# A four-layer mixer kernel: VectorE's y and z first in a step, ScalarE's high part of z before the exponential, chunk-end scaling one step sooner in the last steps

## The reference

```python
proj = hidden_states @ in_proj_w.T               # gate (8192), x|B|C (10240), dt (128)
hBC  = silu(conv1d(x|B|C, 4 taps, causal) + conv_b)
x, Bm, Cm = hBC as (H=128 heads, P=64), (G=8 groups, N=128), (G=8, N=128)
dt = softplus(dt + dt_bias);  A_dt = -exp(A_log) * dt;  x_dt = x * dt
Lmat   = exp(segment_sum(A_dt))                  # decay inside a chunk of 128 tokens
Y_diag = (Cm Bm^T * Lmat) x_dt                   # within the chunk
states = (Bm * exp(A_last - A_cumsum))^T x_dt    # state at the chunk's end
Y_off  = Cm states_of_previous_chunk * exp(A_cumsum)
y = Y_diag + Y_off + D * x
y = y * rsqrt(mean(y^2) + eps) * norm_w * silu(gate)
out = y @ out_proj_w.T
```

## Time and profile before

| what | value |
|---|---|
| median of 3 runs | 1646.56 us (1642.46 to 1646.75) |
| the profiled execution's own time | 1649.56 us |
| its span | 1647.8 us |
| TensorE matmul busy | 1592.1 us, 97% |
| VectorE busy | 1358.0 us, 82% |
| ScalarE busy | 1281.6 us, 78% |
| GpSimd busy | 801.7 us, 49% |
| one group, from one copy to `m_cb_across` to the next | 171.1 to 173.3 us |

### The profile page before, as it was taken

How to read it: one execution, slowest core, us unless ns; L and a number is a source line. 1 busy time by engine, 2 the same in 40 slices (tenths; PEclk the granted TensorE clock), 3 DMA queues, 4 the chain that set the end, 5 groups by cost and what they waited for, 6 DMA issues and landing times.

```text
span 1647.8 us, 27075 instructions
## 1 busy us (share of the span) xinstructions
PE 1592.1 (97%) x8984; PEld 1305.5 (79%) x8984; DVE 1358.0 (82%) x2199; ACT 1281.6 (78%) x2218; POOL 801.7 (49%) x806
## 2 busy tenths in 40 slices
PE   6999999999999999999999999999999999999988
PEld 5888777788888887888788788888788888888766
DVE  5887886888888888887888887898888888878766
ACT  4454459888989798979987898888888888798842
POOL 3565124554556455545554454544554555454460
PEclk9999999999999999999999999999999999999999
DMA  5320345455565446545555455545554645445321
GB/s 174 120 91 1 111 133 155 143 161 148 140 179 153 146 130 176 155 129 150 170 143 160 135 170 143 173 115 172 152 160 131 166 145 160 144 142 161 116 71 52
DMA packets 186074, 229.56 MB, mean 139 GB/s; under 512 B 22384, under 2 KB 122096, under 8 KB 184272
## 3 DMA queue, kind: packets, MB, share of 16 engines
q1 hardware_dynamic: 185936, 227.84, 46.6%
HBM read 190.02 MB, written 37.75 MB: 138 GB/s over the span
## 4 chain that ended last, share of the span: by engine, by line
PE 43%; DVE 20%; issue 9%; ACT 7%; DMA 7%; SPq 1%; POOL 1%; DVEq 0%; ACTq 0%; POOLq 0%
PE bank L160 8%; PE bank L162 7%; PE bank L161 7%; DVE m_xc L1955 7%; PE bank L2343 4%; PE bank L2347 4%; PE bank L2309 4%; PE bank L2344 4%; DMA m_x_rows<-x_turned_rows 4%; DMA x_turned_rows<-m_x_blocks 3%; DVE m_gate L1955 3%; ACT m_mt L1661 2%; DVE m_y L2047 2%; PE bank L2331 2%; DVE xdt L2000 1%
## 5 line engine op out<-in xcount | busy, mean ns | idle before, releaser
L160 PE MATMUL bank<-xh,w_h 128*128 128x512 f32 x1152 | 463.4, 402 | 6.9 <-DVE m_xc L1955 3.9
L162 PE MATMUL bank<-xh,w_l 128*128 128x512 f32 x1152 | 450.9, 391 | 0.0
L161 PE MATMUL bank<-xl,w_h 128*128 128x512 f32 x1152 | 450.5, 391 | 0.0
L1569 POOL TENSOR_TENSOR m_z_l<-m_zg,m_z_h 128x512 fp32r<-128x512 f32 x128 | 179.4, 1401 | 458.2 <-ACT m_z_h L1715 458.2
L1551 POOL TENSOR_TENSOR w_l<-w_raw,w_h 128x512 fp32r<-128x512 f32 x142 | 203.6, 1434 | 228.2 <-ACT w_h L1629 228.2
L1661 ACT ACTIVATE m_mt<-m_mt,m_unit 128x128 f32<-128x128 f32 x1024 | 312.3, 390 | 0.0
L160 PEld LDWEIGHTS bank<-xh,w_h 128*128 128x128 f32 x1152 | 217.1, 188 | 61.9 <-issue 18.9
L162 PEld LDWEIGHTS bank<-xh,w_l 128*128 128x128 f32 x1152 | 216.9, 188 | 46.1
L1955 DVE SCALAR_TENSOR_TENSOR m_xc<-bank,m_par_slots,m_xc 128x1020 f32<-128x1020 f32 (+2 forms) x192 | 243.9, 1270 | 9.9 <-ACT m_xc L1640 5.4
L161 PEld LDWEIGHTS bank<-xl,w_h 128*128 128x128 f32 x1152 | 217.4, 189 | 40.4
L2343 PE MATMUL bank<-m_wo_h,m_z_h 128*128 128x512 f32 x512 | 205.0, 400 | 9.2 <-ACT m_z_h L1715 8.6
(11 more groups left out here) (315 smaller groups left out, 2857.2 us busy)
## 6 DMA issues: line engine op xcount, KB each, us to landing
m_mt<-ncs_rows SPq DMA_DIRECT2D x128, 512.0 KB, 5.8
w_raw<-w_in SPq DMA_DIRECT2D x144, 256.0 KB, 4.2
x_turned_rows<-m_x_blocks SPq DMA_DIRECT2D x120, 256.0 KB, 3.9
m_x_rows<-x_turned_rows SPq DMA_DIRECT2D x480, 64.0 KB, 2.3
m_wo_raw<-w_out_in SPq DMA_DIRECT2D x64, 256.0 KB, 3.9
m_e<-ecs_rows SPq DMA_DIRECT2D x128, 128.0 KB, 3.7
a_wo_raw<-wo_in SPq DMA_DIRECT2D x8, 1024.0 KB, 5.0
x<-x_in SPq DMA_DIRECT2D x8, 256.0 KB, 4.3
```

What stands on the lines that cost most here:

```text
L160: nc.tensor.matmul(out, ah, bh, start=first, stop=False)
L161: nc.tensor.matmul(out, ah, bl, start=False, stop=False)
L162: return nc.tensor.matmul(out, al, bh, start=False, stop=last)
L1569: nc.gpsimd.tensor_tensor(z_l[:, s % 2, :, :], zg[:], f(z_h[:, s % 2, :, :]), ALU.subtract).then_inc(zl_ready, 1)
```

## The change

Three orders are changed; no instruction is added or taken away.

1. VectorE's step: the order was `times_dt`, first `turn_blocks`, `add_out`, then `make_y` and `make_z`. Now it is first `turn_blocks`, `make_y` and `make_z`, `add_out`, `times_dt`.
2. ScalarE's step: `decay` is split in `clamp` (the eight Relu) and `decay` (the exponential). In paired steps other than t = 1 the order is clamps, (in step 15 the copy to `m_cb_across`,) high part of z, square of y, exponential. Before it was clamps, exponential, (copy,) square, high part. In all steps the high part now comes before the square.
3. GpSimd's step: in the last eight steps of the last group `to_chunk_end` for an even step is called at the end of the odd step before it.

```diff
@@ gpsimd step
-                if s % 2 == 0 and own(kind):
+                if s % 2 == 0 and own(kind) and paired(kind, s):
                     to_chunk_end(g, s)
+                if s % 2 == 1 and turned_by_tensor(kind, s):
+                    to_chunk_end(g, s + 1)
@@ scalar
-            def decay(g, s):
+            def clamp(g, s):
                 g, s = g + s // STEPS, s % STEPS
                 half, t = divmod(s, NT)
                 act.wait_ge(rows_loaded[s % ROW_BUFS], (g * (STEPS // ROW_BUFS) + (s // ROW_BUFS + 1)) * 16)
...
                 last.then_inc(clamped, 1)
+
+            def decay(g, s):
+                g, s = g + s // STEPS, s % STEPS
                 act.wait_ge(clamped, at(g, s))
                 slot = mt[:, s % ROW_BUFS, :, :]
                 nc.scalar.activation(slot, slot, ACT.Exp, scale=-1.0).then_inc(decay_ready, 1)
@@
             def square_and_high(g, s):
+                act.wait_ge(z_ready, at(g, s))
+                act.wait_ge(out_done, at(g, s - 2))
+                nc.scalar.activation(z_h[:, s % 2, :, :], zg[:], ACT.Copy).then_inc(zh_ready, 1)
                 act.wait_ge(y_ready, at(g, s))
                 act.wait_ge(sq_summed, at(g, s - 1))
                 nc.scalar.activation(ysq[:], y[:], ACT.Square).then_inc(sq_ready, 1)
-                act.wait_ge(z_ready, at(g, s))
-                act.wait_ge(out_done, at(g, s - 2))
-                nc.scalar.activation(z_h[:, s % 2, :, :], zg[:], ACT.Copy).then_inc(zh_ready, 1)
@@ scalar step
-                if ahead(kind, s + 2) and not (kind == "lead" and s == STEPS - 1):
+                clamps = ahead(kind, s + 2) and not (kind == "lead" and s == STEPS - 1)
+                if clamps:
+                    clamp(g, s + 2)
+                if clamps and not (paired(kind, s) and t != 1):
                     decay(g, s + 2)
...
                 if kind == "lead" and s == STEPS - 1:
+                    clamp(g, s + 2)
                     decay(g, s + 2)
                 if paired(kind, s) and t != 1:
                     for made in made_in(kind, s):
                         square_and_high(g, made)
+                    if clamps:
+                        decay(g, s + 2)
@@ vector step
+                for made in turned_in(kind, s)[:1]:
+                    turn_blocks(g, made)
+                if paired(kind, s):
+                    for made in made_in(kind, s):
+                        make_y(g, made)
+                        make_z(g, made)
+                if behind(kind, s - 2):
+                    add_out(g, s - 2)
                 for made in scaled_first(kind, s):
                     times_dt(g, made)
-                for made in turned_in(kind, s)[:1]:
-                    turn_blocks(g, made)
-                if behind(kind, s - 2):
-                    add_out(g, s - 2)
...
-                if paired(kind, s):
-                    for made in made_in(kind, s):
-                        make_y(g, made)
-                        make_z(g, made)
```

## The result

The changed kernel takes 1680.56 us in the median of 4 runs (1678.34 to 1685.84), the kernel before in the same comparison 1644.51: a ratio of 1.0225 (95% interval 1.0203 to 1.0247), 36 us slower. The forecast was 1624.7, with a range to 1638.0. It is wrong in sign. The profiled execution took 1679.41 us; its span is 1677.7 against 1647.8.

What follows compares the result with a forecast made beforehand. TensorE, busy 97% of the span, was taken as the bound, so only its waits could be won: 10.5 + 1.5 + 3.4 + 11.0 = 26.4 won, 3.5 + 1 given back, 21.9 less, 1624.7 us; range 1617.5 to 1638.

Steps and rivals of the forecast that it cites:

- GpSimd's part: Last eight steps: m_xdd made sooner ends across's waits, slow clock and waits for low parts of output weights, 11.0 us won.
- The waits for z's high and low part and of line 2397: TensorE's waits in add_up and the product within the chunk go: 10.5, 1.5 and 3.4 us won.
- The stretch at clock 0.50 in the tail: Sign: TensorE's slow clock from 1570 to 1572, behind 3.06 us of idling, goes; 1.0 us won.
- ScalarE's wait before the copy: Sign in step 15: ScalarE's wait for across rises from 2.31 to about 4.6 us.
- the mask of step 15: Sign: VectorE's mask in step 15 waits about 3.5 us for the exponential.
- the 1.38 us of drain: Skill's rule on ScalarE's table loads: step 15 dearer by 1.4 us a group, sum 10 us smaller; set aside.
- the second point of "What becomes later": Steps 0, 4, 8: two xdt side by side expose the read, yet diag's second half is in time; nothing, at most 0.5 x 7.
- SyncE's queue holds the weight loads behind that read 2.7 us longer: Steps 0, 4 and 8: the loads are held several steps before they are used; cost nothing.
- over 2 us a group: Sign of a wrong forecast: gaps of that size in diag or the projection.
- the last line: Steps other than 15: exponential 1.2 us later, its mask at VectorE's step end, diag a step or more after; nothing.
- Slower: Rival, 0.07: step 15's exponential holds VectorE, transposes wait for DMA, step 3's xdt over 3.9 us a group late.
- Step 15 bites: Rival, 0.20: late mask reaches diag of step 3 nearly unreduced, costing 16 us instead of 3.5; 1637.2.

Runs made afterwards that it cites:

- e4: The kernel before with only GpSimd's chunk-end scaling one step sooner in the last steps: 1635.71 us, ratio 0.9932.
- e14: The changed kernel with xdt first in VectorE's step and the exponential back right behind the clamps in every step: 1622.01 us, ratio 0.9861.
- e5: The changed kernel with xdt moved to the head of VectorE's step, ahead of transposes, y, z and add_out: 1621.93 us, ratio 0.9861.
- e15: The changed kernel with SyncE's four loads of output weights at t = 2 ahead of the read of x: 1664.50 us, ratio 1.0116.
- e16: e12 with SyncE's four loads of output weights at t = 2 ahead of the read of x: 1653.47 us, ratio 1.0045.
- e1: The changed kernel with VectorE's old order back, ScalarE's and GpSimd's new orders kept: 1632.65 us, ratio 0.9912.
- e10: The changed kernel with the exponential back behind the clamps in every step, z's high part still before the square: 1651.20 us, ratio 1.0029.
- e2: The changed kernel with the exponential of step 15 back ahead of the copy to m_cb_across: 1671.86 us, ratio 1.0147.
- e12: The changed kernel with xdt first in VectorE's step in steps 0, 4 and 8 only: 1668.32 us, ratio 1.0143.
- e3: The kernel before with VectorE's new order alone: 1666.04 us, ratio 1.0113.
- e13: The changed kernel with xdt first in VectorE's step in steps 2, 6, 10, 12 and 14 only: 1642.97 us, ratio 0.9981.

## Why the prediction was wrong

What was won came as forecast, where xdt keeps its place. GpSimd's part: 11.0 forecast, 10.7 measured (e4). The waits for z's high and low part and of line 2397, 15.4 us together: e14 against e4 gives 13.7, and e5 13.8. The stretch at clock 0.50 in the tail is gone, ScalarE's wait before the copy rose from 2.31 to 3.25 (4.6 forecast), the mask of step 15 waits 3.41 (3.5). The table load in its new place takes 1.28 us and the exponential starts 1.29 after it, so the 1.38 us of drain of the Trainium skill's "ScalarE: Activation LUTs", "What ACT_TABLE_LOAD costs", doesn't show here either.

The step that failed is the second point of "What becomes later": "It still fits, by half a microsecond: nothing, at most 0.5 x 7", and behind it "SyncE's queue holds the weight loads behind that read 2.7 us longer, several steps before they are used: nothing". Four things were missed.

First, each delay was added alone to the timeline of the kernel before. The room of 0.5 us held for the second `xdt` of step 4 if the first one was only 2.7 us later against TensorE. It was to be finished 1.8 us behind the start of `add_up` (650.7 against 648.92), and TensorE needs it 4.0 behind (12 x 0.23 + 0.35 + 0.9); it was finished 6.4 behind (662.83 + 1.37 against 657.82). The gap of `diag` is 2.44 instead of none. Of the 4.6 us between 1.8 and 6.4, 2.4 were there before the step began: its mask starts 5.4 us ahead of `add_up` (652.42) instead of 7.8 (641.11), behind the late mask of step 15, the exposed read of step 0 and the transpose of step 3; how much each of them gave is not shown. In step 3 the gap is 1.22 (1.43 in the weight loads, where the earlier trace rows has 0.30); 0.5 to 1 was forecast, and "over 2 us a group" was named as the sign of failure: the sum over a group is beyond that.

Second, the lengths of VectorE's rows were taken from the kernel before. They make the other 2.2 of the 4.6 us: from the start of the mask to the end of the second `xdt` 9.6 us were forecast (641.11 to 650.7), and it took 11.8: the second instruction of `make_y` and both `xdt` are 0.95, 1.10 and 0.61 us longer while GpSimd runs, and the rest is a little shorter. e15 shows the same chain with the transpose of step 3 waiting 0.76 us instead of 2.81: the mask starts 5.7 us ahead of `add_up`, the chain takes 11.8 us again, and the gap is 2.20. What these longer rows cost over the run was tried by no kernel.

Third, the loads behind the read were asked when they are needed, not what they run into. They ran into the write of x, on which VectorE's transposes wait: 15 to 16 us by e15 and e16.

Fourth, the last line: the exponential "1.2 us later in other steps", set down as nothing. It is nothing in two rows of the table (e1 against e4, e5 against e14) and 29 us in the changed one (e10). The mask stands ahead of the y, z and xdt of the next step in VectorE's order; where the waits for the read have used up VectorE's slack, a later mask reaches TensorE. VectorE's busy time speaks for waiting and against longer rows as the way in which it costs: 1390.1 us in e10 and 1385.6 in the changed kernel. It was seen for step 15 and not for the others, though step 15 is 8.7 of the 29 (e2).

The rival that came nearest is "Slower": its path (VectorE held by the exponential, its transposes waiting for DMA behind it, the next xdt late) is there, but its place, step 15, holds 9 us and not the 27 to 35 it needed (by the sum itself, 25.4 / 7 = 3.6 us a group would have been enough, not 3.9); for that step alone 8.7 lies between the 3.5 of the sum and the 16 of "Step 15 bites". "Slower" was given 0.07 because VectorE waited 1.82 us in step 0. VectorE is 83% busy here, and slack in one step was taken for slack in all.

What stays open: the four causes overlap, so they can't be added, and the last 31 us between e16 and e5 are explained by no single run. The longer rows of VectorE are seen in the traces alone: a kernel in which GpSimd makes its low parts a little later would show what they cost. In e12 the weight loads of the projection wait 41.4 us in 84 waits, 14 more than in the changed kernel, so taps are late too; that was not tried apart. Nor was a second buffer for the rows of x.

## What to carry to other kernels

In a loop through DRAM (xdt releases the read, the read releases the next xdt) the first instruction of the loop goes to the head of its engine's step; the work to be hidden behind the transfer goes behind it. Here that one call is worth 59 us, and with it the forecast gain of y and z first is there: 1621.9, or 1620.8 with the exponential of step 15 in its old place, 1.4 to 1.5% below the kernel before. Where a transfer is held back by a wait, look in the same queue at what stands behind it, and which critical transfer the held ones will then run into. Walk several small delays through a group together: each had room, their sum had none. And when an instruction moves, look at what the other engines run at its new place: its length may not be the old one.

## What was not expected of the hardware

Some of VectorE's instructions are longer while GpSimd works. In the whole trace of the changed kernel an instruction of `xdt` takes 0.42 us where no GpSimd row overlaps it (112 of them) and 1.09 where one does for over half of its length (84); the second instruction of `make_y` takes 0.69 and 1.43 (6 and 36 of them). The transposes, which read one tile, take 0.70 and 0.71 (48 and 61), and `add_out`, which reads a tile and a bank, 0.68 either way.

A write of 256 KB takes 2.4 us where the loads ahead of it were issued 3.7 to 7.8 us before (e5), and 5.1 us where they were issued 0.3 to 4.9 us before (the changed kernel); over its whole run the writes take 2.0 to 6.9 us.

A gap of 2.4 to 2.5 us of TensorE, at the same place of the program, had a clock of 0.50 behind it in the fourth group and 1.00 in the third; of the six such gaps three are followed by the low clock. e3, with TensorE waiting 2.27 us for z's high part in the third group, has the low clock behind it there; its window:

```profile
652.00:654.00 2.00, 2.00 (x5) 1.61 (x6) 0.47 (x1) 2.00 (x4) 1.95 (x2) 0.50 0.69 181
```

And waits of an engine say little of what they cost. In the groups between the first copy to `m_cb_across` and the last, VectorE's waits of over 3 us before xdt sum to 76 us in the changed kernel and to 78 in e13, which is 38 us faster.
